# Selective scan: three slots for the broadcast rows of B and C, with a semaphore for each

## The chip, the cores and the metric

The kernel runs on one core of one Trainium2 chip. The metric is the device time of one execution in microseconds (us), the median of three runs. A core has five engines that run side by side and meet through semaphores: TensorE (PE in the rows, PEld for its weight loads), VectorE (DVE), ScalarE (ACT), GpSimd (POOL) and SyncE (SP), which here only issues transfers. Matmul results lie in PSUM, in eight banks of 128 x 512 float32; everything else lies in SBUF.

## What is computed

The program is a decoder of two layers with six blocks, each ending in a residual sum and a layer norm. The change lies in the second block, a selective scan (its inner length 512, state size 16, four batches), and nothing outside it is touched:

```
def step(state, inp):
    d, b, c, u = inp
    dA = jnp.exp(d[..., None] * A)
    state = state * dA + (d * u)[..., None] * b[:, None, :]
    y = jnp.einsum('bdn,bn->bd', state, c)
    return (state, y)
...
_, ys = jax.lax.scan(step, state0, (dt_t, B_t, C_t, u_t))
y = jnp.moveaxis(ys, 0, 2)
y = y + D[None, :, None] * x
y = y * silu(z)
```

So for each of 16 states n, B's row n is multiplied with d*u, a recurrence runs along the 512 positions, and its result is multiplied with C's row n and summed over n.

## The kernel before

The program is five stages that follow each other, each a loop over the four batches (a loop of two turns with two batches written out in each, `c = 2 * i + p`). The first stage holds linear attention and the selective scan together, so the attention's projections and small products are laid between the scan's steps.

**Units.** The scan of a batch is cut into 32 units. Unit U takes one tile of 128 of the 512 channels (`et`) and two states; two units in turn (e = 0 and 1) share the same two states and differ in the channel tile. Such a pair is numbered w = U // 2, 16 pairs to a batch. In this text P(U), S(U), T(U) and Y(U) are the four steps of a unit, named here:

- P(U), GpSimd, line 1388: `h = du * Bb`, one product of 128 x 1024, into one of HR = 4 slots of `h`. It increments `dBu_ready`.
- S(U), VectorE, line 1095: two scans of 128 x 512, which read the decay from PSUM banks 6 and 7 (ScalarE's exponentials, line 838) and `h` from SBUF.
- T(U), VectorE, line 1100: `h = h * Cb`, one product of 128 x 1024 with both inputs in SBUF. It increments `hC_ready`.
- Y(U), TensorE, lines 587 and 588: the two halves of `h` are added into a PSUM bank by matmuls with the identity. It increments `y_added`.

**What each waits for.** P(U) writes the slot that unit U - 4 used, so it waits for Y(U - 4). S(U) waits for P(U) and the exponentials, T(U) for S(U), Y(U) for T(U). Engines take their instructions in the order written, so S, T and VectorE's other steps form one chain: products of keys (`kp`, line 1070, units 0, 1, 3 and 4), masks of the attention state (`kvb`, `ksb`, units 13 and 15), the normaliser (`zr`, unit 17), the gate of the attention output (`xT`, units 20 and 22) and the attention's layer norm (units 24 to 30; its small power step runs on GpSimd ahead of P(28) and P(30)). TensorE runs the attention's projections ahead of some Y: those of keys and values up to unit 7, state products at 12 and 14, the output projection at 23, 25 and 27.

**The broadcasts.** P needs two rows of B copied to all partitions, T two rows of C. SyncE issues two transfers of 512 KB for a pair w, into slot w % 2 of `Bb` and `Cb`. Both count on one semaphore of the slot, and both wait until T of the pair that had the slot is done:

```
sp.wait_ge(hC_ready, START + after(c, NU, max(0, 2 * (w - 1))))
sp.dma_start(Bb[:, w % 2, :, :], bc_dram[bass.ds(c, 1), 0, 2 * q:2 * q + 2, :]
```

`hC_ready` at 2(w - 1) of the batch means that T of pairs 0 to w - 2 is done. GpSimd waits for the slot's full count, so for C as well as B, though it reads B alone.

Of the kernel before, what the change touches and what calls it, by code (L numbers as in the profile page):

```python
# [21 lines left out]
ALU = mybir.AluOpType  # L22
# [3 lines left out]
P = 128  # L26
B, S, D = 4, 512, 512
# [20 lines left out]
UNITS = B * XH  # L48
UL = NIDX // UNITS // P
HR = 4  # L50
SBUF_END = 229344
LN_EPS = 1e-5
START = 1
# [3 lines left out]
def after(c, per, k):  # L57

    return c * per + k
# [21 lines left out]
def build(nc, io, stages=5):  # L81
    x_in, out = io["x"], io["out"]
    bc_dram = nc.dram_tensor("bc_dram", [B, 2, NST, S], F32).ap()
# [3 lines left out]
    with ExitStack() as ctx:  # L87
        sems = []

        def sem(name):  # L90
            sems.append(ctx.enter_context(nc.semaphore(name)))
            return sems[-1]
# [106 lines left out]
        s1 = Space(nc, shared_end)  # L199
# [10 lines left out]
        ctxT = s1("ctxT", [P, KC, S])  # L210
        xpad = s1("xpad", [P, KI, S + KW - 1])
        u = s1("u", [P, KI, S]); dt = s1("dt", [P, KI, S]); du = s1("du", [P, KI, S])
        Bb = s1("Bb", [P, 2, 2, S]); Cb = s1("Cb", [P, 2, 2, S])
        h = s1("h", [P, HR, 2, S]); yacc = s1("yacc", [P, KI, S])
        xdbl = s1("xdbl", [DTR + 2 * NST, S])
        qp = s1("qp", [P, KD, S])
# [15 lines left out]
        A_exp = sem("A_exp"); A_neg = sem("A_neg"); pads_set = sem("pads_set")  # L232
        conv_step = sem("conv_step"); conv_done = sem("conv_done"); u_ready = sem("u_ready")
        xdbl_full = sem("xdbl_full"); xdbl_copied = sem("xdbl_copied"); xdbl_stored = sem("xdbl_stored")
        b_loaded = [sem("b_loaded0"), sem("b_loaded1")]
        sp_e = sem("sp_e"); sp_l = sem("sp_l"); sp_d = sem("sp_d"); sp_s = sem("sp_s")
        sp_a = sem("sp_a"); dt_ready = sem("dt_ready"); du_ready = sem("du_ready")
        neg_ready = sem("neg_ready"); qk_ready = sem("qk_ready"); v_ready = sem("v_ready")
# [6 lines left out]

        NU = (NST // 2) * KI
        NW = NST

        def unit_of(U):

# [111 lines left out]
        def _(sp):  # L362
# [32 lines left out]
            with sp.Fori(0, B // 2) as i:  # L395
                for p in range(2):
                    c = 2 * i + p
                    sp.wait_ge(conv_done, START + after(c, KI, 0))
                    load_x(c, p, x_in)
                    sp.dma_start(ctxT[:, :, :], io["ctxT"][bass.ds(c, 1), :, :].rearrange("a (k p) s -> p (a k) s", p=P))\  # L400
                        .then_inc(ctx_loaded, 16)
                    sp.wait_ge(xdbl_copied, START + c + 1)
                    sp.dma_start(bc_dram[bass.ds(c, 1), :, :, :].rearrange("a e n s -> (a e n) s"),
                                 xdbl[DTR:DTR + 2 * NST, :]).then_inc(xdbl_stored, 16)
                    sp.wait_ge(xdbl_stored, START + 16 * (c + 1))
                    hold(sp)
                    for w in range(NW):
                        q = w % (NST // 2)
                        sp.wait_ge(hC_ready, START + after(c, NU, max(0, 2 * (w - 1))))
                        sp.dma_start(Bb[:, w % 2, :, :], bc_dram[bass.ds(c, 1), 0, 2 * q:2 * q + 2, :]  # L410
                                     .rearrange("a n s -> (a n) s").partition_broadcast(P)).then_inc(b_loaded[w % 2], 16)
                        sp.dma_start(Cb[:, w % 2, :, :], bc_dram[bass.ds(c, 1), 1, 2 * q:2 * q + 2, :]
                                     .rearrange("a n s -> (a n) s").partition_broadcast(P)).then_inc(b_loaded[w % 2], 16)
            if stages >= 2:
                sp.wait_ge(stored, STORED0 + 16 * B)
                simple_stage(1, rows_of)
# [4 lines left out]
            if stages >= 4:  # L421
# [13 lines left out]
                with sp.Fori(0, B // 2) as i:  # L435
                    for p in range(2):
                        c = 2 * i + p
# [23 lines left out]
        def _(pe):  # L461
# [30 lines left out]
            with pe.Fori(0, B // 2) as i:  # L492
                for p in range(2):
# [61 lines left out]
                    for U in range(NU):  # L555
# [28 lines left out]
                        if q == 0 and et >= 2:  # L584
                            pe.wait_ge(y_sum, START + after(c, KI, e + 1))
                        pe.wait_ge(hC_ready, START + after(c, NU, U + 1))
                        pe.matmul(bank[4 + e][:, :], ident[:, :], h[:, U % HR, 0, :], start=(q == 0), stop=False)  # L587
                        pe.matmul(bank[4 + e][:, :], ident[:, :], h[:, U % HR, 1, :], start=False, stop=(q == NST // 2 - 1))\  # L588
                            .then_inc(y_added, 1)
# [435 lines left out]
        def _(dve):  # L1025
# [27 lines left out]
            with dve.Fori(0, B // 2) as i:  # L1053
                for p in range(2):
                    c = 2 * i + p
# [32 lines left out]
                    def unit(U):  # L1088

                        w, q, et, e = unit_of(U)  # L1090
                        s = U % HR
                        dve.wait_ge(dBu_ready, START + after(c, NU, U + 1))
                        for n in range(2):
                            dve.wait_ge(dA_ready, START + after(c, 2 * NU, 2 * U + n + 1))
                            dve.tensor_tensor_scan(h[:, s, n, :], bank[6 + n][:, :], h[:, s, n, :], 0.0,  # L1095
                                                   ALU.mult, ALU.add).then_inc(scanned, 1)
                        if e == 0:
                            dve.wait_ge(b_loaded[w % 2], START + after(c, 32 * NW // 2, 32 * (w // 2 + 1)))
                        dve.wait_ge(scanned, START + after(c, 2 * NU, 2 * U + 2))
                        dve.tensor_tensor(h[:, s, :, :], h[:, s, :, :], Cb[:, w % 2, :, :], ALU.mult).then_inc(hC_ready, 1)  # L1100

                    def y_total(et):
                        dve.wait_ge(y_added, START + after(c, NU, (et // 2 + 1) * NU // 2 - 1 + et % 2))
# [43 lines left out]
            if stages >= 2:  # L1147
# [18 lines left out]
                with dve.Fori(0, B // 2) as i:  # L1166
                    for p in range(2):
                        c = 2 * i + p
# [19 lines left out]
            if stages >= 3:  # L1188
                dve.wait_ge(stage_loaded[2], START + L0[2])
                with dve.Fori(0, B // 2) as i:  # L1190
                    for p in range(2):
                        c = 2 * i + p
# [53 lines left out]
            if stages >= 4:  # L1246
# [31 lines left out]
                with dve.Fori(0, B // 2) as i:  # L1278
                    for p in range(2):
                        c = 2 * i + p  # L1280
# [30 lines left out]
                        for hh in range(XH):  # L1311
                            for t in range(NT):
                                n = 4 * hh + t
# [7 lines left out]
                            for t in range(NT):  # L1321
                                n = 4 * hh + t
# [14 lines left out]
            if stages >= 5:  # L1337
# [6 lines left out]
                with dve.Fori(0, B // 2) as i:  # L1344
                    for p in range(2):
                        c = 2 * i + p
# [12 lines left out]
        def _(pool):  # L1359
# [12 lines left out]
            with pool.Fori(0, B // 2) as i:  # L1372
                for p in range(2):
                    c = 2 * i + p
                    for et in range(KI):
                        pool.wait_ge(dt_ready, START + after(c, KI, et + 1))
                        pool.wait_ge(u_ready, START + after(c, KI, KI))
                        pool.tensor_tensor(du[:, et, :], dt[:, et, :], u[:, et, :], ALU.mult).then_inc(du_ready, 1)

                    def input_of(U):  # L1380

                        w, q, et, e = unit_of(U)
                        if e == 0:
                            pool.wait_ge(b_loaded[w % 2], START + after(c, 32 * NW // 2, 32 * (w // 2 + 1)))
                        if q == 0:
                            pool.wait_ge(du_ready, START + after(c, KI, et + 1))
                        pool.wait_ge(y_added, START + after(c, NU, max(0, U - HR + 1)))
                        pool.tensor_tensor(h[:, U % HR, :, :], du[:, et:et + 1, :].to_broadcast([P, 2, S]),  # L1388
                                           Bb[:, w % 2, :, :], ALU.mult).then_inc(dBu_ready, 1)

                    for U in range(NU):
                        if U in (28, 30):
                            t = (U - 28) // 2
                            ln_pool(pool, after(c, 8, t), t % 2)
                        input_of(U)
                    for t in (2, 3):
                        ln_pool(pool, after(c, 8, t), t % 2)
                    for t in range(NT):
                        ln_pool(pool, after(c, 8, 4 + t), t % 2)
                    store_chunk(0, c)  # L1400
            for n in range(1, min(stages, 5)):
# [4 lines left out]
                with pool.Fori(0, B // 2) as i:  # L1406
                    for p in range(2):
                        c = 2 * i + p
# [87 lines left out]
```

## Time and profile before

| what | us |
|---|---|
| median of 3 runs (3208.7 to 3212.39) | 3208.88 |
| the profiled execution, its own time | 3205.01 |
| its span, first to last instruction | 3203.3 |
| of it, the scans of the four batches, first P to last T | 164.2, 163.1, 163.3, 162.5 |

Times in the rows are microseconds from the span's start unless a column is marked ns. A row of a timeline gives start, duration, engine, line, operation, output<-inputs and a count of merged instructions; in brackets stands how long the engine had been idle and what released it. The four scans make up 653.1 of 3203.3 us. What lies around a span (3205.01 against 3203.3) is not part of any stretch.

### The profile page before, as it was taken

Reading aid. Unit: us, or ns where it says so; the run is one execution under the profiler, and the core shown is the slowest. Engines: PE = TensorE matmul, PEld = TensorE weight load, DVE = VectorE, ACT = ScalarE, POOL = GpSimd, SP = SyncE. Lnnn points to the kernel's source line nnn. Section 1 sums busy time; section 2 is a strip of 40 time slices with the busy share of each in tenths; the row PEclk is TensorE's granted clock in tenths of the full one; section 3 lists DMA queues with packets and bytes.
Section 4 is the critical chain, followed back from the end, with each engine's and each line's share of the span. In section 5 each row is a group of like instructions: output and inputs, shape, how many; then the busy total and the mean of one; then the engine's idle time right before and its main releaser. Section 6 shows DMA issues by size and latency. Waiting matters only on the chain.

```text
span 3203.3 us, 32041 instructions
## 1 busy us (share of the span) xinstructions
PE 2821.5 (88%) x8706; PEld 1484.7 (46%) x8706; DVE 2014.5 (63%) x3867; ACT 1080.1 (34%) x1962; POOL 698.0 (22%) x571
## 2 busy tenths in 40 slices
PE   6788888788748877889999999999999999799998
PEld 2323333233316654445544555455545554456755
DVE  3996996987984436567864788278827884311111
ACT  4335325325323221135542555055514553100100
POOL 1552553543530115521101101011101110100000
PEclk9988988898978889999999999999999999899999
DMA  3231321321330120310012000200020003200000
GB/s 111 92 112 46 106 93 67 105 85 66 113 136 27 39 72 32 145 35 17 14 36 71 17 14 25 81 14 17 18 79 24 17 17 119 88 27 1 26 13 13
DMA packets 76589, 178.75 MB, mean 56 GB/s; under 512 B 9107, under 2 KB 25747, under 8 KB 75414
## 3 DMA queue, kind: packets, MB, share of 16 engines
q1 hardware_dynamic: 65526, 139.71, 13.3%
q0 software_dynamic: 5472, 21.01, 1.7%
q10 hardware_dynamic: 5440, 16.32, 1.5%
q8 instruction: 58, 0.95, 0.1%
q14 instruction: 93, 0.76, 0.1%
HBM read 147.32 MB, written 29.69 MB: 55 GB/s over the span
## 4 chain that ended last, share of the span: by engine, by line
PE 56%; DVE 22%; issue 9%; DMA 5%; POOL 4%; ACT 2%; SPq 1%; DVEq 1%; POOLq 0%; ACTq 0%
PE bank L465 44%; PE bank L740 7%; DVE h L1095 5%; DMA Cb<-bc_dram 3%; PE bank L698 3%; DVE sm L1315 2%; POOL h L1388 2%; DVE h L1100 2%; DVE p L1326 1%; PE bank L683 1%; DVE val L1267 1%; DVE kp L1070 1%; DVE val L1275 1%; DVE kt L1300 1%; DVE at L1233 1%
## 5 line engine op out<-in xcount | busy, mean ns | idle before, releaser
L1388 POOL TENSOR_TENSOR h<-du,Bb 128x1024 f32<-128x1024 f32 x128 | 345.1, 2717 | 259.8 <-DMA Cb<-bc_dram 251.1
L838 ACT ACTIVATE bank<-dt,A 128x512 f32<-128x512 f32 x256 | 176.8, 691 | 435.2 <-DVE h L1095 435.2
L1095 DVE TENSOR_TENSOR_SCAN h<-bank,h 128x512 f32<-128x512 f32 x256 | 297.7, 1203 | 15.2 <-POOL h L1388 15.1
L587 PE MATMUL bank<-h,ident 128*128 128x512 f32 x256 | 159.7, 709 | 126.4 <-DVE h L1100 126.3
L961 ACT ACTIVATE p<-bank,sm,rq 128x512 f32<-128x512 f32 x256 | 199.0, 777 | 212.8 <-DVE sm L1319 212.8
L174 DVE TENSOR_TENSOR rsum<-bank,xc 128x512 f32<-128x512 f32 x64 | 44.1, 688 | 355.1 <-PE bank L740 222.9
L188 POOL TENSOR_SCALAR rstd<-mv 128x1 f32<-128x1 f32 x96 | 33.3, 347 | 1010.4 <-DVE mv L182 1010.4
L1447 POOL TENSOR_TENSOR rq<-rq,mhalf 128x4 f32<-128x4 f32 x64 | 65.6, 1025 | 796.2 <-DVE rq L1306 796.2
L465 PE MATMUL bank<-pT,v 128*128 128x512 f32 x512 | 232.8, 598 | 3.2 <-ACT pT L783 3.2
L1100 DVE TENSOR_TENSOR h<-h,Cb 128x1024 f32<-128x1024 f32 x128 | 229.0, 1789 | 8.8
L465 PE MATMUL bank<-xT,wxq 128*128 128x512 f32 x512 | 230.6, 593 | 3.5 <-ACT xT L783 3.5
L465 PE MATMUL bank<-kr,q 128*128 128x512 f32 x512 | 230.6, 593 | 0.0
L740 PE MATMUL bank<-woh,oT 128*128 128x512 f32 x512 | 222.4, 594 | 4.9 <-ACT oT L783 3.6
L1315 DVE TENSOR_REDUCE sm<-bank 128x1 f32<-128x512 f32 x256 | 176.5, 690 | 33.9 <-PE bank L465 33.9
L1275 DVE COPY_PREDICATED val<-msk,val 128x258 f32<-128x258 int32 x448 | 173.4, 448 | 29.0 <-DVE val L1275 12.2
L1353 DVE TENSOR_TENSOR h<-bank,sg 128x512 f32<-128x512 f32 (+1 forms) x44 | 30.4, 691 | 228.1 <-PE bank L465 228.1
L1267 DVE TENSOR_SCALAR val<-msk,lx,le 128x258 uint32<-128x258 uint32 x512 | 171.6, 410 | 2.3
L740 PEld LDWEIGHTS bank<-woh,oT 128*128 128x128 f32 x512 | 96.4, 190 | 130.8 <-issue 113.3
L465 PEld LDWEIGHTS bank<-pT,v 128*128 128x128 f32 x512 | 97.8, 192 | 126.5 <-issue 121.9
L465 PE MATMUL bank<-wdn,h 128*128 128x512 f32 (+1 forms) x352 | 152.2, 593 | 3.1 <-DVE h L1353 3.1
L465 PEld LDWEIGHTS bank<-xT,wxq 128*128 128x128 f32 x512 | 96.9, 190 | 125.0 <-issue 120.5
L588 PE MATMUL bank<-h,ident 128*128 128x512 f32 x256 | 152.8, 683 | 0.0
(190 smaller groups left out, 5036.9 us busy)
## 6 DMA issues: line engine op xcount, KB each, us to landing
Bb<-bc_dram SPq DMA_DIRECT2D x64, 512.0 KB, 3.5
Cb<-bc_dram SPq DMA_DIRECT2D x64, 512.0 KB, 4.8
x_dram<-xo POOLq DMA_DIRECT2D x16, 1024.0 KB, 4.7
xc<-x_dram SPq DMA_DIRECT2D x16, 1024.0 KB, 5.4
woh<-in_Wo SPq DMA_DIRECT2D x64, 256.0 KB, 2.6
idx<-in_idx SPq DMA_DIRECT2D x64, 129.0 KB, 2.1
w_dram<-val SPq DMA_DIRECT2D x64, 129.0 KB, 2.4
xc<-in_x SPq DMA_DIRECT2D x4, 1024.0 KB, 7.8
```

The costliest lines, as they stand in the source:

```text
L465: m = pe.matmul(dst, l, r, start=(k == 0), stop=(k == len(pairs) - 1))
L587: pe.matmul(bank[4 + e][:, :], ident[:, :], h[:, U % HR, 0, :], start=(q == 0), stop=False)
L588: pe.matmul(bank[4 + e][:, :], ident[:, :], h[:, U % HR, 1, :], start=False, stop=(q == NST // 2 - 1))\
L740: m = pe.matmul(bank[4 + t][:, :], oT[:, hh, t * P:(t + 1) * P], woh[:, hh % 2, :], start=(hh == 0), stop=(hh == XH - 1))
L838: act.activation(bank[6 + n][:, :], dt[:, et, :], ACT.Exp, scale=A[:, et, 2 * q + n:2 * q + n + 1]).then_inc(dA_ready, 1)
L961: act.activation(p4[:, t, :], bank[4 + t][:, :], ACT.Exp, bias=sm4[:, 4 + t:5 + t], scale=rq[:, hh % 2, 1, t:t + 1], accum_out=sm4[:, 8 + ...
L1095: dve.tensor_tensor_scan(h[:, s, n, :], bank[6 + n][:, :], h[:, s, n, :], 0.0, ALU.mult, ALU.add).then_inc(scanned, 1)
L1100: dve.tensor_tensor(h[:, s, :, :], h[:, s, :, :], Cb[:, w % 2, :, :], ALU.mult).then_inc(hC_ready, 1)
L1267: dve.tensor_scalar(val[:, j, :].bitcast(U32), msk[:, 0, :].bitcast(U32), lx[:, j:j + 1], le[:, j:j + 1], ALU.bitwise_and, ALU.bitwise_xor ...
L1275: dve.copy_predicated(val[:, s, :], msk[:, b, :], val[:, s + (1 << (b - 1)), :]).then_inc(lut_step, 1)
L1315: dve.tensor_reduce(sm4[:, t:t + 1], bank[4 + t][:, :], AX.X, ALU.max).then_inc(max_ready, 1)
L1388: pool.tensor_tensor(h[:, U % HR, :, :], du[:, et:et + 1, :].to_broadcast([P, 2, S]), Bb[:, w % 2, :, :], ALU.mult).then_inc(dBu_ready, 1)
```

## The change

`Bb` and `Cb` get three slots (BR = 3) in place of two. The six slots have a semaphore each. The transfer of B for pair w waits for `dBu_ready` (GpSimd's products of pairs 0 to w - 3 are done) in place of `hC_ready`; that of C waits for `hC_ready` of pairs 0 to w - 3. GpSimd waits for B's semaphore alone, VectorE's T for C's alone. Nothing is computed otherwise than before, and no instruction on TensorE or ScalarE changes.

```
+BR = 3
...
-        Bb = s1("Bb", [P, 2, 2, S]); Cb = s1("Cb", [P, 2, 2, S])
+        Bb = s1("Bb", [P, BR, 2, S]); Cb = s1("Cb", [P, BR, 2, S])
...
-        b_loaded = [sem("b_loaded0"), sem("b_loaded1")]
+        b_loaded = [sem(f"b_loaded{n}") for n in range(BR)]; c_loaded = [sem(f"c_loaded{n}") for n in range(BR)]
...
+        def loads_in(slot):
+
+            return 16 * ((NW - slot + BR - 1) // BR)
...
-                        sp.wait_ge(hC_ready, START + after(c, NU, max(0, 2 * (w - 1))))
-                        sp.dma_start(Bb[:, w % 2, :, :], bc_dram[bass.ds(c, 1), 0, 2 * q:2 * q + 2, :]
-                                     .rearrange("a n s -> (a n) s").partition_broadcast(P)).then_inc(b_loaded[w % 2], 16)
-                        sp.dma_start(Cb[:, w % 2, :, :], bc_dram[bass.ds(c, 1), 1, 2 * q:2 * q + 2, :]
-                                     .rearrange("a n s -> (a n) s").partition_broadcast(P)).then_inc(b_loaded[w % 2], 16)
+                        sp.wait_ge(dBu_ready, START + after(c, NU, max(0, 2 * (w - BR + 1))))
+                        sp.dma_start(Bb[:, w % BR, :, :], bc_dram[bass.ds(c, 1), 0, 2 * q:2 * q + 2, :]
+                                     .rearrange("a n s -> (a n) s").partition_broadcast(P)).then_inc(b_loaded[w % BR], 16)
+                        sp.wait_ge(hC_ready, START + after(c, NU, max(0, 2 * (w - BR + 1))))
+                        sp.dma_start(Cb[:, w % BR, :, :], bc_dram[bass.ds(c, 1), 1, 2 * q:2 * q + 2, :]
+                                     .rearrange("a n s -> (a n) s").partition_broadcast(P)).then_inc(c_loaded[w % BR], 16)
...
-                            dve.wait_ge(b_loaded[w % 2], START + after(c, 32 * NW // 2, 32 * (w // 2 + 1)))
+                            dve.wait_ge(c_loaded[w % BR], START + after(c, loads_in(w % BR), 16 * (w // BR + 1)))
                         dve.wait_ge(scanned, START + after(c, 2 * NU, 2 * U + 2))
-                        dve.tensor_tensor(h[:, s, :, :], h[:, s, :, :], Cb[:, w % 2, :, :], ALU.mult).then_inc(hC_ready, 1)
+                        dve.tensor_tensor(h[:, s, :, :], h[:, s, :, :], Cb[:, w % BR, :, :], ALU.mult).then_inc(hC_ready, 1)
...
-                            pool.wait_ge(b_loaded[w % 2], START + after(c, 32 * NW // 2, 32 * (w // 2 + 1)))
+                            pool.wait_ge(b_loaded[w % BR], START + after(c, loads_in(w % BR), 16 * (w // BR + 1)))
...
-                                           Bb[:, w % 2, :, :], ALU.mult).then_inc(dBu_ready, 1)
+                                           Bb[:, w % BR, :, :], ALU.mult).then_inc(dBu_ready, 1)
```

SyncE's queue of the first turn of the loop, before, at the transfers of pair 2 (the first that waits for a slot) and the wait of pair 3; `hC_ready` counts T:

```order
L409 REGISTER_ALU
L410 ISA [waits hC_ready]
L410 DMA Bb<-bc_dram 128x1024
L412 ISA
L412 DMA Cb<-bc_dram 128x1024
```

The same queue of the changed kernel at the transfers of pair 3 (the first that waits for a slot there):

```order
L414 REGISTER_ALU
L415 ISA [waits dBu_ready]
L415 DMA Bb<-bc_dram 128x1024
L418 ISA [waits hC_ready]
L418 DMA Cb<-bc_dram 128x1024
```

No transfer has moved past another; the one wait ahead of the two has become one ahead of each, the first on GpSimd's products, the second on VectorE's. The B of the next pair stands behind the C of this one in the queue.

GpSimd's queue before, over three pairs late in a batch:

```order
L1387 REGISTER_ALU [waits b_loaded0]
L1388 TENSOR_TENSOR h<-du,Bb 128x1024 [waits y_added]
L1387 REGISTER_ALU
L1388 TENSOR_TENSOR h<-du,Bb 128x1024 [waits y_added]
L1387 REGISTER_ALU [waits b_loaded1]
L1388 TENSOR_TENSOR h<-du,Bb 128x1024 [waits y_added]
```

The same of the changed kernel:

```order
L1393 REGISTER_ALU [waits b_loaded1]
L1394 TENSOR_TENSOR h<-du,Bb 128x1024 [waits y_added]
L1393 REGISTER_ALU
L1394 TENSOR_TENSOR h<-du,Bb 128x1024 [waits y_added]
L1393 REGISTER_ALU [waits b_loaded2]
L1394 TENSOR_TENSOR h<-du,Bb 128x1024 [waits y_added]
```

The order of the products is the same, and each still waits for `y_added`, that is for Y four units back; only the slot's semaphore differs, and its name now stands for B alone.

## Rows read from the trace of the kernel before

**Rows 1.** The page's costliest groups (busy us, mean ns, idle before): P and T.

```profile
L1388 POOL TENSOR_TENSOR h<-du,Bb 128x1024 f32<-128x1024 f32 x128 | 345.1, 2717 | 259.8 <-DMA Cb<-bc_dram 251.1
...
L1100 DVE TENSOR_TENSOR h<-h,Cb 128x1024 f32<-128x1024 f32 x128 | 229.0, 1789 | 8.8
```

**Rows 2.** The list of waits: us in total, times, longest us.

```profile
POOL h L1388 <- DMA Cb<-bc_dram: 251.1, 54, 9.8
DVE h L1095 <- POOL h L1388: 15.1, 4, 3.8
```

**Rows 3.** Second batch's scan: us, busy PE, PEld, DVE, ACT, POOL, PEclk, DMA, GB/s.

```profile
303.50:466.60 163.10, 132.13 (x273) 50.85 (x272) 156.47 (x132) 52.80 (x80) 91.73 (x41) 0.87 0.29 100
```

**Rows 4.** Line 1100, T: shortest, median and longest duration in ns.

```profile
L1100 DVE TENSOR_TENSOR h<-h,Cb x128: 1224/1226/3349, 81.8 to 917.0; 128x1024 f32<-128x1024 f32 x128
```

**Rows 5.** Timeline of VectorE, second batch: T(7), S(8), T(8), T(9), T(11).

```profile
345.37 3.17 DVE L1100 TENSOR_TENSOR h<-h,Cb 128x1024 f32<-128x1024 f32 x1
348.46 2.32 DVE L1095 TENSOR_TENSOR_SCAN h<-bank,h 128x512 f32<-128x512 f32 x2
350.89 1.23 DVE L1100 TENSOR_TENSOR h<-h,Cb 128x1024 f32<-128x1024 f32 x1
...
354.39 2.87 DVE L1100 TENSOR_TENSOR h<-h,Cb 128x1024 f32<-128x1024 f32 x1
...
363.12 3.16 DVE L1100 TENSOR_TENSOR h<-h,Cb 128x1024 f32<-128x1024 f32 x1
```

**Rows 6.** Timeline of GpSimd in the same stretch: P(8) and P(9).

```profile
345.11 2.34 POOL L1388 TENSOR_TENSOR h<-du,Bb 128x1024 f32<-128x1024 f32 x1 [6.90 <-DMA Cb<-bc_dram]
...
347.41 3.33 POOL L1388 TENSOR_TENSOR h<-du,Bb 128x1024 f32<-128x1024 f32 x1
```

**Rows 7.** Timeline of TensorE, second batch: Y(9), then Y(11).

```profile
357.32 1.12 PE L587 MATMUL bank<-h,ident 128*128 128x512 f32 x2 [1.25 <-DVE h L1100]
358.28 1.02 PE L588 MATMUL bank<-h,ident 128*128 128x512 f32 x2
...
366.34 2.08 PE L587 MATMUL bank<-h,ident 128*128 128x512 f32 x2 [3.46 <-DVE h L1100]
368.21 1.91 PE L588 MATMUL bank<-h,ident 128*128 128x512 f32 x2
```

**Rows 8.** Timeline, third batch: the end of Y(23), and P(27).

```profile
660.96 0.59 PE L588 MATMUL bank<-h,ident 128*128 128x512 f32 x1
...
661.63 2.80 POOL L1388 TENSOR_TENSOR h<-du,Bb 128x1024 f32<-128x1024 f32 x1 [0.89 <-PE bank L588]
```

**Rows 9.** Timeline: T(29) and P(31) of the third batch.

```profile
681.59 1.26 DVE L1100 TENSOR_TENSOR h<-h,Cb 128x1024 f32<-128x1024 f32 x1
681.73 3.34 POOL L1388 TENSOR_TENSOR h<-du,Bb 128x1024 f32<-128x1024 f32 x1
```

**Rows 10.** Timeline: P(31) and T(29) of the fourth batch.

```profile
905.47 2.34 POOL L1388 TENSOR_TENSOR h<-du,Bb 128x1024 f32<-128x1024 f32 x1
...
905.77 3.11 DVE L1100 TENSOR_TENSOR h<-h,Cb 128x1024 f32<-128x1024 f32 x1
```

**Rows 11.** The page's transfers: KB each, us from issue to landing.

```profile
Bb<-bc_dram SPq DMA_DIRECT2D x64, 512.0 KB, 3.5
Cb<-bc_dram SPq DMA_DIRECT2D x64, 512.0 KB, 4.8
```

**Rows 12.** Timeline of VectorE, second batch: the product of keys behind T(0).

```profile
311.49 2.83 DVE L1070 TENSOR_TENSOR kp<-er 128x512 f32<-128x512 f32 x1
```

**Rows 13.** Timeline, second batch: T(22), Y(23), and T(31).

```profile
421.30 1.23 DVE L1100 TENSOR_TENSOR h<-h,Cb 128x1024 f32<-128x1024 f32 x1
...
433.66 1.13 PE L587 MATMUL bank<-h,ident 128*128 128x512 f32 x2
434.62 1.02 PE L588 MATMUL bank<-h,ident 128*128 128x512 f32 x2
...
465.36 1.23 DVE L1100 TENSOR_TENSOR h<-h,Cb 128x1024 f32<-128x1024 f32 x1
```

## The prediction, made before the changed kernel ran

> **What bounds the kernel now.** I read the page first. It puts GpSimd's product P at 345.1 us busy and 251.1 us idle behind the transfer of C, and the list of waits says the same in 54 waits [rows 1, 2]. That looks like 251 us to be won. But GpSimd is not the engine that sets the pace. The table of stretches has VectorE busy for 156.47 of 163.10 us of the second batch's scan, GpSimd for 91.73 [rows 3]. And VectorE starved for a product only once a batch, 15.1 us in all, at the first unit, before any slot has to be given back [rows 2]. So the transfers' lateness reaches the time only through something that lengthens VectorE's own instructions.
>
> The timeline shows what that is. A free T takes 1.23 us (the shortest 1.224, the median 1.226), yet the mean is 1.789 and the longest 3.349 [rows 1, 4]. T(7) was issued at 345.37 and took 3.17; P(8) had started at 345.11 and ended at 347.45, and T(7) ended 1.09 later [rows 5, 6]. P(9) stood ready at 347.41, waited for T(7) and ended at 350.74, 2.20 after T(7)'s end. The scans S(8) beside it took their usual 2.32, and T(8), issued at 350.89, found GpSimd idle and took 1.23 [rows 5, 6]. So P and T exclude each other, whoever asks first goes first, and S runs beside P. Two products landing together, as now, cost one collision a pair: T(7) ends at 348.54, T(9) at 357.26 [rows 5], 8.72 us for two units, where two free units take 7.1 (3.57 each: S 2.32, T 1.23). The blocked time in T is 229.0 - 128 x 1.226 = 72 us over the four batches, 18 a batch.
>
> The Trainium skill ("SBUF — State Buffer", § Who interferes with whom) says that a VectorE instruction with two SBUF inputs contends with a GpSimd instruction that reads SBUF, and that issue order decides who blocks. By that rule, the rows above agree.
>
> **The change, part by part.** The extra waits on SyncE and the split semaphores cost nothing: SyncE has nothing else in its queue during the scan. The transfers land 3.5 and 4.8 us after issue [rows 11]. With three slots, C of pair w is issued after T(2w - 5), five units ahead of its use, at least 17 us. B of pair w + 1 stands behind that C in the queue, and its product P(2w + 2) waits for Y(2w - 2), three units later, at least 10 us. Both are hidden by the units between; if that cover failed, a product would be no later than it is now. So GpSimd's 251 us behind the transfer goes to near zero.
>
> What is late next is Y: P(U) waits for Y(U - 4). The four matmuls of Y(9) start 0.06 after T(9)'s end and end 2.04 after it (358.28 + 1.02 - 357.26); after an idle 3.46 us at a granted clock at its low level the same four took until 3.84 after T(11) [rows 5, 7]. P starts 0.09 after Y where it waits for it (661.63 against 661.55) [rows 8]. So a freed P asks at 2.13 after T's end. The next T asks at 2.28 (odd units) or 2.35 (even): S overlaps T's end by 0.08 and takes 2.32, and so on [rows 5]. **The product now arrives 0.15 to 0.22 us ahead of the next T**, the worst place: T then ends at 2.13 + 2.34 + 1.08 = 5.55. That is 5.55 a unit against 4.36 now. How fine this race is, two batches show: T(29) issued 0.14 before P(31) took 1.26, and 0.30 after it took 3.11 [rows 9, 10].
>
> Against that, TensorE idles 5.55 - 2.04 = 3.5 us in such a unit, and after 3.46 us Y came at 3.84 [rows 7]. Then P asks at 3.93, T has gone at 3.50. Three units follow, ending at 3.50, 7.34 (T blocked until P ends at 6.27) and 12.9 (blocked again): 4.3 a unit. Where TensorE's projections delay Y, P also falls anywhere in the cycle.
>
> I walked the second batch with these rules, and its other work left at its lengths:
>
> - Units 0 to 11. P(4) now starts at 315.5 in place of 323.5 and blocks T(1) for 1.1. T(3) is blocked instead of the key product behind it. The key products are blocked anyway (2.83 us [rows 12]) and take up the differences. T(11) ends at 366.7 against 363.12 + 3.16 = 366.28 [rows 5]: +0.4.
> - Units 12 to 22. With Y(11) late, T(12), T(15) and T(16) go free, and T(17), T(18) are blocked less: T(22) ends at 420.4 against 422.53 [rows 13]: -2.5. With Y(11) in time it is +0.6.
> - Units 23 to 31, counted from T(22)'s end. P(26) no longer waits for its transfer; it runs from 2.5 to 4.85 and T(23), asking at 3.5, ends at 5.9. The output projection holds Y(23) until 434.62 + 1.02 - 422.53 = 13.1 [rows 13], so P(27) starts at 13.2, just ahead of T(25) at 13.5, which ends at 16.6. P(28) waits for the norm's power step and blocks T(26); P(30) or P(31) blocks T(28) or the norm behind it. T(31) ends at 47.8 after T(22), against 465.36 + 1.23 - 422.53 = 44.06 [rows 13]: +3.7.
>
> The sum for a batch is +1.6 by the first way and +4.7 by the second; I take +2, near the first, since the row nearest to the case (3.46 us idle) has the low clock. Four batches: +8 us. The sum is against the profiled 3205.01, and is carried over to the median 3208.88: **3217 us**.
>
> The Trainium skill ("Perfetto Trace Analysis", § Identifying Performance Opportunities) reads a gap that repeats, on the engine that should be saturated, as a possible shortage of buffers. GpSimd's repeated gap invites that reading; by it up to its 251 us would be the prize, by the rows above none of it, since VectorE is the saturated one.
>
> **The rivals.**
>
> - *Products fall behind T (faster).* If Y mostly comes later than 2.28 after T, as in 3.84 [rows 7], each P starts behind T and runs under S, and T is free. At the bound the whole blocked time but that of the first unit (1.9 a batch) would go: 72 - 8 = 64 us, 3145. For it: GpSimd needs 2.34 + 1.2 us of each 3.57, which just fits; VectorE has no other loss. Against it: Y is early whenever TensorE is warm and free, and 4.3 a unit is little under 4.36. An eighth to a half of the bound is what I can see, -8 to -30 us: 3179 to 3201. Chance 0.24.
> - *The race locks ahead of T (clearly slower).* Decides from the point where Y takes 2.04 in most units. Then 14 units a batch without projections ahead (8 to 11, 13 to 22 in part) take 5.55 for 4.36: 14 x 1.19 = 17 a batch, 67 in all at the bound, 3276; a third to a half of it gives 3230 to 3245. For it: Y(9) and others are at 2.04. Against: the idle that it makes lowers the clock. Chance 0.17.
> - *A wash.* The collisions only change places: -1.5 to +1 a batch, 3203 to 3213. Chance 0.19. That the change does not do what it says (the transfer still binds) has no way here; it would give the same time.
> - *My forecast*, +1 to +4 a batch, 3213 to 3225: chance 0.40.
>
> **How the numbers follow.** A measurement of this kernel tells about 0.2% from no change, 6.4 us: 3202.5 to 3215.3. Faster: the first rival, and a little of the wash, 0.25. Same: most of the wash and the lower edge of my own case, 0.27. Slower: the rest of it and the lock, 0.48. The range leaves out the far tenth on each side: 3188 to 3246; my own case alone is 3213 to 3225.
>
> **What would show it right or wrong.** In the profile after: P's idle behind a transfer gone but for the batch's start, and put down to Y (lines 587, 588) in its place; T's mean duration still near 1.8 us, not 1.23; T(23) and T(25) longer than 2 us in most batches, where they are short now; the four scans 163 to 168 us each; later stages unchanged. A mean of T under 1.5 would make the first rival right, one over 2.1 the second. I am wrong if the walk's ties (several within 0.1 us) fall one way together, since all batches run the same program.

## The result, and the profile after

| | median us | runs, us |
|---|---|---|
| before | 3208.88 | 5 runs, 3200.59 to 3212.39 |
| changed | 3223.63 | 5 runs, 3221.10 to 3228.78 |

The ratio is 1.0052, with a 95% interval of 1.0034 to 1.0070: slower by half a per cent, 11 to 22 us. The profiled execution is the slowest of its five, 3228.78 us, its span 3227.1, so the two traces differ by 23.8 us, more than the medians do (14.8). Times here and below are of fast executions; one more of E7, at 3984.37 us and a granted clock of 0.682, was slow and is left out.

The page's groups for P and T after the change (busy us, mean ns, idle before and its releaser), which answer to [rows 1]:

```profile
L1394 POOL TENSOR_TENSOR h<-du,Bb 128x1024 f32<-128x1024 f32 x128 | 331.3, 2601 | 285.6 <-PE bank L594 285.4
...
L1106 DVE TENSOR_TENSOR h<-h,Cb 128x1024 f32<-128x1024 f32 x128 | 246.2, 1924 | 9.5 <-DVE h L1101 0.9
```

GpSimd no longer waits for any transfer. It waits 285.4 us for the second half of Y (line 594 is 588 moved by six lines) where it had waited 251.1 for the transfer. T's mean rose from 1.789 to 1.924 us; its blocked time (what T took beyond its free 1.226 us) is 246.2 - 128 x 1.226 = 89 us, 17 more than before. Of the 128 T, 35 were issued at most 0.35 us behind a product's start, where 20 were before.

The table of stretches, one row for each batch's scan from the first P to the last T (us, busy time by engine, granted clock, DMA share, GB/s), to be read beside [rows 3]:

```profile
76.70:244.10 167.40, 130.86 (x273) 50.50 (x273) 159.70 (x132) 52.78 (x80) 87.32 (x41) 0.88 0.28 91
305.30:474.70 169.40, 131.35 (x272) 50.06 (x272) 161.27 (x132) 52.79 (x80) 86.57 (x41) 0.88 0.27 90
541.70:710.60 168.90, 130.99 (x272) 50.52 (x271) 160.85 (x132) 52.79 (x80) 87.95 (x41) 0.89 0.27 90
771.30:942.30 171.00, 134.40 (x273) 51.22 (x272) 162.75 (x132) 52.79 (x80) 85.61 (x41) 0.87 0.24 80
```

The scans take 3.2, 6.3, 5.6 and 8.5 us more than before, 23.6 in sum: the difference of the spans but for 0.2 us. VectorE's busy time grew by 4.8 of the second batch's 6.3 us, with the same instructions. Work was added to no engine.

T's 17 us are not the whole account. VectorE's time in the four scans, by what it wrote (durations summed; the last row is busy time):

| | before, us | changed, us | difference |
|---|---|---|---|
| T (`h`, 128 instructions) | 229.0 | 246.2 | +17.2 |
| key products (`kp`, 16) | 36.7 | 19.5 | -17.2 |
| masks of the attention state (`ksb`, 16) | 11.1 | 20.4 | +9.3 |
| the norm's last step (`xo`, 16) | 8.7 | 16.5 | +7.8 |
| all of VectorE | 627.1 | 644.6 | +17.5 |

What T lost, the key products gave back: 12 of the 16 were shut out before, 4 after. The loss that is left lies in the masks and the norm's last step, and in about 6 us of longer waits. The masks before and after (shortest, median, longest in ns):

```profile
L1118 DVE TENSOR_SCALAR ksb<-hmask,bank x16: 220/224/2110, 148.9 to 839.9; 128x16 f32<-128x16 f32 x16
...
L1124 DVE TENSOR_SCALAR ksb<-hmask,bank x16: 222/1512/2183, 151.3 to 856.2; 128x16 f32<-128x16 f32 x16
```

A mask is a product of an SBUF tile with one value per partition. All ten that took over 1.4 us in the changed kernel were issued while a product P ran.

The timeline of the second batch shows where. VectorE's T(20), T(21) and T(22), and GpSimd's P(22) and P(23) (one merged row), P(24) and P(25):

```profile
413.16 3.33 DVE L1106 TENSOR_TENSOR h<-h,Cb 128x1024 f32<-128x1024 f32 x1
...
419.97 2.35 DVE L1106 TENSOR_TENSOR h<-h,Cb 128x1024 f32<-128x1024 f32 x1
...
424.67 3.19 DVE L1106 TENSOR_TENSOR h<-h,Cb 128x1024 f32<-128x1024 f32 x1
```

```profile
413.06 5.65 POOL L1394 TENSOR_TENSOR h<-du,Bb 128x1024 f32<-128x1024 f32 x2 [8.74 <-PE bank L594]
418.88 2.35 POOL L1394 TENSOR_TENSOR h<-du,Bb 128x1024 f32<-128x1024 f32 x1 [0.17 <-PE bank L594]
424.44 2.34 POOL L1394 TENSOR_TENSOR h<-du,Bb 128x1024 f32<-128x1024 f32 x1 [3.21 <-PE bank L594]
```

P(22) starts 0.10 us ahead of T(20), P(25) 0.23 ahead of T(22). Both T take over 3.1 us; T(20) and T(22) took 1.23 before [rows 13 for T(22)]. P(25) is the plain case: it was released by Y(21), which ended 2.04 us after its own T(21). P(22) is not. Y(18) had stood behind eight matmuls of the attention (from 403.91 to 409.56 us; the list of TensorE's work given above with the units leaves out those ahead of Y(16), Y(18), Y(20) and Y(21)) and ended 5.7 us after T(18). That this fell 2.2 us after T(19), just ahead of T(20), comes from that work and not from the 2.13 us of the prediction.

TensorE's timeline, same batch: Y(10), then the output projection behind Y(22).

```profile
364.98 1.47 PE L593 MATMUL bank<-h,ident 128*128 128x512 f32 x2 [3.60 <-DVE h L1106]
366.24 1.91 PE L594 MATMUL bank<-h,ident 128*128 128x512 f32 x2
```

```profile
431.49 4.80 PE L471 MATMUL bank<-wo,xT 128*128 128x512 f32 x8
```

After 3.60 us of idle Y(10) ran mostly at the low clock (a granted clock of 0.60 over the four matmuls) and ended 3.2 us after its T; Y(11) was back at 2.30. Behind 3.56 us of idle and Y(22) the output projection ran at a granted clock of 0.75 and took 4.80 us, where it took 3.60 before, and the norm's first sum waited 1.33 us for it. Such a wait came in three of the four batches, 4.0 us in sum, and before in none.

### The profile page after: what moved, and what is told of

Its sections match the earlier page's. It is cut to its first block, busy times and chain, and to the rows that moved or that the text cites. A ratio compares the mean times of both kernels' runs of the same rounds, so it can differ in the third digit from the quotient of the medians.

```text
span 3227.1 us, 32065 instructions
## 1 busy us (share of the span) xinstructions
PE 2823.7 (87%) x8706; PEld 1485.0 (46%) x8706; DVE 2032.3 (63%) x3867; ACT 1079.6 (33%) x1962; POOL 675.8 (21%) x571
## 4 chain that ended last, share of the span: by engine, by line
PE 56%; issue 16%; DVE 15%; POOL 9%; ACT 2%; DMA 1%; SPq 0%; DVEq 0%; POOLq 0%; ACTq 0%
PE bank L471 43%; POOL h L1394 7%; PE bank L746 6%; PE bank L704 3%; DVE sm L1321 2%; DVE p L1332 1%; PE bank L689 1%; DVE val L1273 1%; DVE h L1101 1%; DVE val L1281 1%; DVE kt L1306 1%; DVE st L180 1%; DVE rsum L175 1%; DVE at L1239 1%; PE bank L682 1%
## 5 line engine op out<-in xcount | busy, mean ns | idle before, releaser
L1394 POOL TENSOR_TENSOR h<-du,Bb 128x1024 f32<-128x1024 f32 x128 | 331.3, 2601 | 285.6 <-PE bank L594 285.4
L1101 DVE TENSOR_TENSOR_SCAN h<-bank,h 128x512 f32<-128x512 f32 x256 | 297.9, 1204 | 15.9 <-POOL h L1394 15.1
L593 PE MATMUL bank<-h,ident 128*128 128x512 f32 x256 | 171.2, 755 | 131.8 <-DVE h L1106 131.8
L1106 DVE TENSOR_TENSOR h<-h,Cb 128x1024 f32<-128x1024 f32 x128 | 246.2, 1924 | 9.5 <-DVE h L1101 0.9
L1453 POOL TENSOR_TENSOR rq<-rq,mhalf 128x4 f32<-128x4 f32 x64 | 65.5, 1024 | 796.5 <-DVE rq L1312 796.5
L594 PE MATMUL bank<-h,ident 128*128 128x512 f32 x256 | 156.1, 696 | 0.0
```

Source lines behind the costliest of these rows:

```text
L1106: dve.tensor_tensor(h[:, s, :, :], h[:, s, :, :], Cb[:, w % BR, :, :], ALU.mult).then_inc(hC_ready, 1)
```

## The experiments

Each was timed beside the kernel before on the same chip; its median there was 3204.3 us in the first group (E1 to E4), 3207.1 in the second (E5 to E8) and 3208.3 in the third (E9 to E12). Ratios are against the kernel before, with a 95% interval.

### E1. The early release of B without the third slot

```
-BR = 3
+BR = 2
```

> The changed kernel with BR = 2: the early release of B and the split semaphores alone, without the third slot. Theory (products become free of the transfers, bound by Y, and land in front of the next T): B of a pair is issued at least four products ahead even with two slots and C is needed three units after its issue, so GpSimd is as free of the transfers as with three slots; time as the changed kernel, 3218 to 3230, T's mean near 1.92 us. Rival (the third slot is what frees the products): GpSimd waits for transfers again and the time is that of before, 3205 to 3212.

Measured: 3217.6 us, ratio 1.0037 (1.0024 to 1.0050). T's mean is 1.948 us. The median is 0.4 us under the range I gave, the kernel is slower than before, and GpSimd waits for Y (266.4 us in 72 waits) and not for a transfer (0.6 us, once). The rival is out: the third slot isn't needed for the transfers to drop out.

### E2. The third slot without the early release

```
-                        sp.wait_ge(dBu_ready, START + after(c, NU, max(0, 2 * (w - BR + 1))))
+                        sp.wait_ge(hC_ready, START + after(c, NU, max(0, 2 * (w - BR + 1))))
...
-                        sp.wait_ge(hC_ready, START + after(c, NU, max(0, 2 * (w - BR + 1))))
...
-                                     .rearrange("a n s -> (a n) s").partition_broadcast(P)).then_inc(c_loaded[w % BR], 16)
+                                     .rearrange("a n s -> (a n) s").partition_broadcast(P)).then_inc(b_loaded[w % BR], 16)
...
-                            dve.wait_ge(c_loaded[w % BR], START + after(c, loads_in(w % BR), 16 * (w // BR + 1)))
+                            dve.wait_ge(b_loaded[w % BR], START + after(c, 2 * loads_in(w % BR), 32 * (w // BR + 1)))
...
-                            pool.wait_ge(b_loaded[w % BR], START + after(c, loads_in(w % BR), 16 * (w // BR + 1)))
+                            pool.wait_ge(b_loaded[w % BR], START + after(c, 2 * loads_in(w % BR), 32 * (w // BR + 1)))
```

> Three slots, but one semaphore for B and C of a slot and both transfers behind hC_ready: the third slot alone. Theory: the transfers are again issued early enough, products wait for Y and not for a transfer, time as the changed kernel, 3218 to 3230. Rival (B's slot given back by GpSimd's product, and its wait ahead of C's, is what costs): 3205 to 3212.

Measured: 3229.0 us, ratio 1.0066 (1.0048 to 1.0084), T's mean 1.933 us, GpSimd behind Y for 283.9 us. So either half of the change, alone, makes the products free of the transfers and the kernel slower. The two halves share no line; what they have in common is that a product is now released by Y.

### E3. The change, with P(U) waiting for T(U - 2) as well

```
                         pool.wait_ge(y_added, START + after(c, NU, max(0, U - HR + 1)))
+                        pool.wait_ge(hC_ready, START + after(c, NU, max(0, U - 1)))
```

> The changed kernel with one more wait ahead of each product: P(U) also waits for hC_ready of T(U - 2). Theory (only the moment at which P asks costs): P asks 0.1 us after a T has ended, runs under the scans, ends 2.43 after that T, when the next T asks at 2.28 to 2.35 and loses nothing (1.08 in place of 1.22 after the wait). Blocked time in T falls from 89 us to under 15, the key products and T(0) go free too: 3110 to 3145, T's mean 1.25 to 1.35. Rival (GpSimd's idle time and run-ahead are what the kernel needs): products come later than now, VectorE's scans wait for them, time over 3224.

Measured: 3159.1 us, ratio 0.9855 (0.9840 to 0.9869): 45 us faster than before by an added wait. The timeline of VectorE (T(14), S(15) and T(15)), and of GpSimd (P(16)):

```profile
356.13 1.23 DVE L1106 TENSOR_TENSOR h<-h,Cb 128x1024 f32<-128x1024 f32 x1
357.27 2.33 DVE L1101 TENSOR_TENSOR_SCAN h<-bank,h 128x512 f32<-128x512 f32 x2
359.64 1.23 DVE L1106 TENSOR_TENSOR h<-h,Cb 128x1024 f32<-128x1024 f32 x1
```

```profile
357.44 2.34 POOL L1395 TENSOR_TENSOR h<-du,Bb 128x1024 f32<-128x1024 f32 x1 [4.02 <-DVE h L1106]
```

P(16) starts 0.08 us after T(14)'s end, runs under the scans, and T(15) takes its free 1.23 us. Over all units T's mean is 1.304 us, as expected. The time, though, is 14 us above the range I gave: of 72 + 17 us blocked, 79 went and the key products gained 9 more, but 63 arrived in the time by the ratios (71 between the two profiled executions). Two places took the rest back. TensorE's projections ahead of Y(7) now hold P(11), and VectorE waits for it, 2.3 us a batch. And the power step of the norm stands between products that wait longer; the timeline at unit 26 shows P(27), the two power steps, P(28) and the norm's last step:

```profile
408.68 2.35 POOL L1395 TENSOR_TENSOR h<-du,Bb 128x1024 f32<-128x1024 f32 x1 [3.70 <-PE bank L594]
411.00 1.20 POOL L189 TENSOR_SCALAR rstd<-mv 128x1 f32<-128x1 f32 x1
412.28 0.57 POOL L191 TENSOR_TENSOR rstd<-rstd,mhalf 128x1 f32<-128x1 f32 x1
412.82 2.34 POOL L1395 TENSOR_TENSOR h<-du,Bb 128x1024 f32<-128x1024 f32 x1
412.96 2.49 DVE L196 TENSOR_SCALAR xo<-rsum,mv,rstd 128x512 f32<-128x512 f32 x1 [0.84 <-POOL rstd L191]
```

The last step of the norm waits 0.84 us for GpSimd and is then shut out by P(28), which was issued 0.14 us ahead of it. In the changed kernel this happened once a batch, here twice.

### E4. The kernel before, with the same added wait

```
                         pool.wait_ge(y_added, START + after(c, NU, max(0, U - HR + 1)))
+                        pool.wait_ge(hC_ready, START + after(c, NU, max(0, U - 1)))
```

> The kernel before (two slots, one semaphore, both behind hC_ready) with the same added wait of P(U) for T(U - 2). Theory: the odd products of a pair start behind T, but the first of a pair still waits for its transfer, which lands 5.3 us after T(2w - 3), that is 1.7 into the next unit, and blocks one T a pair: gain only at the batch's start, where T(0) and the key product go free, 3165 to 3200, T's mean 1.6 to 1.75. Rival (the transfers do not matter at all): the same time as the changed kernel with this wait.

Measured: 3162.0 us, ratio 0.9859 (0.9842 to 0.9876), T's mean 1.535 us. GpSimd waits 139.6 us for T in 73 waits, and 105.9 us for the transfer of C in 41.

The transfer still delays 41 products and T is still blocked for 196.4 - 157 = 39 us, as the theory has it, but the time, 3 us below the range, and T's mean are better than I expected: the time equals E3's within 3 us, though 29 us more of T are blocked. In both, a batch's scan takes 151 to 153 us. What E3 wins in T it loses elsewhere: its norm's last steps take 15 us more than E4's, and VectorE waits 9 us more for products. So with the order at the port put right, the change of this case has hardly an effect left.

### E5. More work on TensorE ahead of `y_added`

```
+                        pe.matmul(bank[4 + e][:, :], ident[:, :], h[:, U % HR, 0, :], start=(q == 0), stop=False)
-                        pe.matmul(bank[4 + e][:, :], ident[:, :], h[:, U % HR, 0, :], start=(q == 0), stop=False)
+                        pe.matmul(bank[4 + e][:, :], ident[:, :], h[:, U % HR, 0, :], start=False, stop=False)
```

> The changed kernel with Y's first identity matmul issued twice (the first half of h is added twice, so y is not the scan's): TensorE has 0.86 us more to do in each unit at its full clock, and y_added comes that much later. Theory (the moment of P's asking costs, not lateness): where Y is free, P asks 3.0 us after T's end in place of 2.13, so the next T (2.28 to 2.35) goes first and P runs under the scans; fewer T are blocked and the kernel is faster than the changed one though an engine has 110 us more work: 3190 to 3218, T's mean 1.5 to 1.8. Rival (the slots of h come free too late, TensorE's latency is what GpSimd waits for and pays): slower than the changed kernel, over 3230.

Measured: 3205.0 us, ratio 0.9997 (0.9987 to 1.0007), T's mean 1.575 us. With 110 us more of matmuls, counted at the full clock, in the chain that GpSimd waits for, the changed kernel lost its half per cent. P now asks behind the next T more often: 13 T were issued at most 0.35 us behind a product's start, in place of 35, and T took 45 us less. Lateness of Y is not free, though. VectorE waited for a product 10 times, 31.0 us, in place of 4 times and 15.1, and the key products took 13 us more. And the added matmuls raised the granted clock in the scans from 0.87-0.89 to 0.96-0.97 (TensorE's busy time grew by 51 us, not 110). So T's mean shows the effect of the order; how much of the gain in time comes from the clock is not separated here.

### E6. Five slots of h

```
-HR = 4
+HR = 5
```

(on the kernel of E1)

> HR = 5 slots of h on top of the version with two slots for B and C, split semaphores and B's early release (five slots and three broadcasts do not fit SBUF together). To be read against that version, 3217.6. Theory: P(U) waits for Y(U - 5) in place of Y(U - 4); the wait is one unit older but has the same phase against T, 2.13 after a T's end, so T is blocked as often: 3208 to 3228, T's mean 1.85 to 2.0. Rival (GpSimd's 285 us of waiting for Y is a shortage of slots, and more slots win it): under 3200, GpSimd's wait for Y clearly under 200 us.

Measured: 3217.0 us, ratio 1.0029 (1.0017 to 1.0042), T's mean 1.923 us. The time is E1's, as the theory said, but GpSimd's wait is not: it fell to 71.8 us behind Y, and 158.6 us behind the transfer of B came in its place. Half of the rival came true, the shorter wait for Y; its time, under 3200, did not. T was blocked as often (58 T over 1.5 us, 56 in E1), and 36 us less of waiting on GpSimd were worth nothing. This kernel doesn't show the phase argument by itself, since the transfer had a share in when P asked, and the transfer also took the place of the shortage, so what five slots are worth with the transfers out of the way is not shown.

### E7. A fill in place of the product

```
-                        pool.tensor_tensor(h[:, U % HR, :, :], du[:, et:et + 1, :].to_broadcast([P, 2, S]),
-                                           Bb[:, w % BR, :, :], ALU.mult).then_inc(dBu_ready, 1)
+                        hold(pool)
+                        pool.memset(h[:, U % HR, :, :], 0.5).then_inc(dBu_ready, 1)
```

> The changed kernel with GpSimd's product replaced by a fill of the same slot with 0.5, behind the same waits (the input of the scan is left out): GpSimd writes SBUF but reads none. Theory (it is the reading of SBUF by P that shuts T out): T's mean 1.23 to 1.30 and its longest under 1.5 whatever moment the fill starts at; time as with the waits for T or a little better, 3135 to 3165. Rival (any GpSimd work beside T blocks it): T is still stretched by the fill's length when the fill starts first, mean over 1.4.

Measured: 3102.9 us, ratio 0.9674 (0.9658 to 0.9691), below the range I gave. (`hold` only adds one to a semaphore.) T over all 128 (shortest, median, longest in ns), and one pair of rows of the timelines, GpSimd's fill and T:

```profile
L1106 DVE TENSOR_TENSOR h<-h,Cb x128: 1224/1225/1226, 79.6 to 814.5; 128x1024 f32<-128x1024 f32 x128
...
124.91 0.95 POOL L1395 MEMSET h<- 128x1024 f32 x1 [0.76 <-PE bank L594]
...
124.92 1.22 DVE L1106 TENSOR_TENSOR h<-h,Cb 128x1024 f32<-128x1024 f32 x1
```

The fill started 0.01 us ahead of T and T was not touched; its longest was 1.226 us, though 41 fills were running when a T started. So T is shut out by the product, which reads SBUF, and not by the fill, which only writes it. Eight key products also ran beside a fill and took 0.68 to 0.69 us; no mask and no last step of the norm met one. The fill is also shorter (0.95 us against 2.34), which makes this a bound and not a fair time: against E3, more than half of the further gain lies between T(22) and T(31), 41.7 us a batch in place of 48.6, which E12 comes to as well. The Trainium skill ("SBUF — State Buffer", § Who interferes with whom) limits the contention of a two-input VectorE instruction to GpSimd instructions that read SBUF; these rows agree.

### E8. The looser wait, for T(U - 3)

```
+                        pool.wait_ge(hC_ready, START + after(c, NU, max(0, U - 2)))
```

> The changed kernel with P(U) waiting also for T(U - 3), one unit looser than the wait for T(U - 2) that gave 3159. Theory: where Y(U - 4) is in time P asks 0.1 us after a T and T is free; where the projections make Y later than that, P asks anywhere and some T are blocked: between the two, 3160 to 3190, T's mean 1.35 to 1.6. Rival (the gain of the tighter wait came from holding GpSimd back by a unit, not from the order at the port): near the changed kernel, over 3205.

Measured: 3165.8 us, ratio 0.9870 (0.9851 to 0.9889), T's mean 1.522 us: inside the theory's ranges, outside the rival's.

### E9, E10, E11. The wait on a third of the units

```
+                        if U <= 11:
+                            pool.wait_ge(hC_ready, START + after(c, NU, max(0, U - 1)))
```

(`12 <= U <= 22` in E10, `U >= 23` in E11)

> The changed kernel with the wait of P(U) for T(U - 2) on units 0 to 11 alone. Theory: with the wait on all units a batch reaches T(11)'s end 11 us sooner after P(0) than the changed kernel (52.0 against 63.0 in the second batch), so this part is worth about 44 us of the 60: 3172 to 3190. Rival (the gain is that of the whole chain and a part gives nothing, since later collisions take it back): over 3210.

> The same wait on units 12 to 22 alone. Theory: T(11) to T(22) takes 50.7 us with the wait on all units against 59.4 in the changed kernel, so about 35 us: 3183 to 3200, below the kernel before. Rival (the middle was no place of loss, as the prediction's walk had it, which put T(22) 2.5 us earlier than before): 3215 to 3228.

> The same wait on units 23 to 31 alone. The wait on all units left this part at 48.9 us from T(22) to T(31) against 46.8 in the changed kernel: the output projection sets Y there and the norm's power step on GpSimd stands behind products that now wait longer. Theory: no gain here, 3218 to 3236. Rival (collisions ahead of T(23) to T(28) cost 3.7 us a batch, as the walk had it, and the wait wins them back): 3205 to 3215.

Measured: E9 3179.3 us, ratio 0.9902 (0.9889 to 0.9915); E10 3197.0 us, 0.9963 (0.9948 to 0.9977); E11 3214.6 us, 1.0023 (1.0012 to 1.0035). Against the changed kernel's 1.0052 the parts give 1.50, 0.89 and 0.29%, 48, 29 and 9 us. E9's gain is as expected. E10's is 29 in place of 35, and its rival's range is out. E11 missed its range by 3 us and lies inside its rival's, at the edge.

The traces say where the gains lie. Mean us a batch in one execution each, from P(0) to T(11)'s end, on to T(22)'s end, on to T(31)'s end:

| | to T(11) | T(11) to T(22) | T(22) to T(31) |
|---|---|---|---|
| before | 62.6 | 55.9 | 44.7 |
| changed | 63.0 | 59.4 | 46.7 |
| E9, wait on 0 to 11 | 54.3 | 56.5 | 47.4 |
| E10, wait on 12 to 22 | 60.9 | 52.0 | 48.5 |
| E11, wait on 23 to 31 | 63.0 | 53.7 | 48.7 |
| E3, wait on all | 52.1 | 50.5 | 48.6 |

E11 wins nothing late in a batch: that part takes 2.0 us more, as its theory had it, and the rival's collisions there are not what the wait wins back. Its gain lies ahead, where P(23) and P(24) now stand behind T(21) and T(22): these took 1.22 to 1.23 us in place of 2.09 to 3.34. The three sum to 86, the whole (E3) to 63, since all three parts count a gain in the middle (2.9, 7.4 and 5.7 us a batch, where the whole wins 8.8). And a gain from the wait does not by itself show that the change had lost there: from P(0) to T(11) the change lost 0.4 us a batch and the wait wins 8.7. That the middle was a place of loss is shown by the traces, 55.9 against 59.4.

### E12. The norm's power step one product earlier

```
-                        if U in (28, 30):
-                            t = (U - 28) // 2
+                        if U in (27, 29, 31):
+                            t = (U - 27) // 2
...
-                    for t in (2, 3):
+                    for t in (3,):
```

(on the kernel of E3)

> The wait for T(U - 2) on all units, and GpSimd's power steps of the attention's layer norm one product earlier (ahead of P(27), P(29) and P(31)). Theory: the norm's last step no longer waits 0.8 us for GpSimd and is no longer shut out by the product that follows the power step (2.49 us in place of 0.55, twice a batch): 3 to 6 us a batch, 3133 to 3150. Rival (that part is bound by the output projection on TensorE anyway): as with the wait alone, 3155 to 3162.

Measured: 3133.5 us, ratio 0.9761 (0.9746 to 0.9775), the fastest version with the whole computation in it: 75 us under the kernel before on its chip, and the rival is out. From T(22) to T(31) a batch took 48.1 to 48.9 us in the trace of E3 and 41.8 to 41.9 in this one. The duration of line 196, the norm's last step (shortest, median, longest in ns), now never shut out:

```profile
L196 DVE TENSOR_SCALAR xo<-rsum,mv,rstd x96: 512/516/549, 196.3 to 3125.6; 128x512 f32<-128x512 f32 x96
```

## Why the prediction was right, and which terms were off

- **VectorE sets the pace, the wait for the transfer is worth nothing by itself.** Right. The wait went completely, in the change and in E1 and E2, and all three are slower.
- **P and T exclude each other by order of asking.** Right, shown by E7 (no reading, no blocking) and E3 (P behind T, T free). But the walk priced T and the key products alone. The masks and the norm's last step are shut out too, 17 us more in the changed kernel; it left the masks out and named the norm once, in place of T(28). That a unit then costs 3.5 us is in E3's rows: T(14) ends at 357.36, T(15) at 360.87.
- **The freed P asks 2.13 us after a T, just ahead of the next.** Right where no attention work stands ahead of Y: P(25) above, the 35 T issued at most 0.35 us behind a product, and T's mean in E5. Its check of the start behind Y, 661.63 against 661.55, is 0.08 us and not 0.09.
- **The transfers stay hidden with the new waits.** Right: no wait for a transfer is left in the changed kernel.
- **Units 0 to 11, +0.4 a batch.** Measured from P(0) to T(11)'s end: 0.15, 0.30, 0.43, 0.80, mean +0.4. It is the rest of two large terms, T +4.7 and key products -4.3 a batch.
- **Units 12 to 22, -2.5 (or +0.6), of which I took the low one.** This is the term that was mis-sized. Measured from T(11) to T(22): +3.4 on average, 59.36 against 55.91. Of this 2.3 are the masks, which the walk left at their lengths, and 0.7 are T, where the walk's whole sum was -2.5. I took Y(11) to be at the low clock, because it was in this batch before. In the changed kernel it was Y(10) that met the low clock, and Y(11) came at 2.30. And the walk names no collision at T(20) and T(22), which the trace of this batch decides by 0.10 and 0.23 us against them.
- **Units 23 to 31, +3.7.** Measured +2.0 on average, 46.68 against 44.67. T(23) and T(25), which I named, took 1.23 us: P(26) came behind T(23), and P(27) behind T(25). T(26) was blocked (2.26 us), yet T as a whole took 1.1 us a batch less than before in this part. The loss came from the norm's last step (2.49 us in place of 0.55, once a batch) and from waits, 1.1 us a batch more, most of it for a projection at a lowered clock. The sum was near, the places were not.
- **The sum, +8 (3217).** The four batches of the profile gave +23.6; the medians of five runs +14.8, by the interval 11 to 22. Of my two ways, +1.6 and +4.7 a batch, the second was the better one: 4 x 4.7 = 19. The way of the change was foreseen from the mechanism. That the size came out as near as it did is in part luck: the middle had the wrong sign, the late part was put too high by 1.7 us a batch, and the masks were left out.
- **The rivals.** A mean of T under 1.5 or over 2.1 was to decide for them; it is 1.92. The other signs: later stages were unchanged, but T(23) and T(25) were not long, and three of the four scans (169.4, 168.9 and 171.0 us) lie above the 163 to 168 that I gave. The wash is out by the interval. The first rival's state, P behind T, is real, but the change does not reach it; it takes E3's wait.

Not separated here: how much of the added blocking is the phase against VectorE's steps and how much the longer idle of TensorE that follows from it. E6 was meant to show the phase alone and did not. The difference between E1 and E2 (3217.6 and 3229.0, intervals that just meet) I leave open; it is not in T, which was blocked 92.4 and 90.5 us, and part of it is in the masks and the norm's last step, each 4 us longer in E2.

## What to carry to other kernels

When two engines exclude each other, a longer wait of the faster one can be a gain: give it a wait that makes it ask right after the slower engine's exclusive instruction, so that it runs beside the part that doesn't collide. Before removing a wait, ask which event becomes the next releaser and at what phase of the bounding engine's cycle it falls; here the transfer's landing happened to be better than the accumulation's end. An idle time of 251 us on an engine with 22% of the span busy says nothing about the kernel's time. And count every instruction of the bounding engine that can be shut out: here the largest group lost 17 us, another won them back, and two small groups made the difference.

## What the runs showed of the hardware

- A product of VectorE with two SBUF inputs that was issued 0.01 to 0.32 us after a GpSimd product, which reads SBUF, took 3.1 to 3.42 us in place of 1.226. Behind a GpSimd fill of the same size it took at most 1.226 (E7).
- The fill of 128 x 1024 float32 took 0.95 us on GpSimd, the product 2.34.
- A blocked instruction restarts cheaply: T ended 1.08 us after P's end, where a free one takes 1.22, so a P that ends 0.1 us into T's wait costs nothing (E3).
- The norm's last step, a VectorE instruction with one SBUF tensor input and per-partition scalars, was shut out by a product too: 2.49 us against 0.55 (E3's rows). So were the masks, of the same kind: up to 2.18 us against 0.22. The walk had no mask in it, and the norm once.
- VectorE's products with one input in PSUM were not: issued while a GpSimd product ran, `xT` took 0.67 to 0.69 us (eight of them) and `kvb` 0.28 (five), their usual lengths (the changed kernel).
